# Splitting a fourth head by batch pairs at the end of each convolution layer, with new ring places for the filters

## What is computed

```python
x = x + moe(_gn(x))                    # 8 experts, top 2, silu(x w1) * (x w3) w2
x = x + conv(_gn(x), w3, w7, w15, w_mix)   # three times, own weights
# conv: y = concat([dwconv(x, w) for w in (w3, w7, w15)], axis=channels)
#       y = y.reshape(b, heads, 96, tokens);  out = einsum('blhm,dm->blhd', y, w_mix)
# _gn: mean and variance over a group of 16 tokens x all 512 channels
```

## Time and profile before

| what | value |
|---|---|
| median of 3 runs | 1033.46 us (1033.12 to 1034.08) |
| the profiled execution's own time | 1034.63 us |
| its span in the profile | 1033.0 us |
| PE busy | 992.5 us (96%) |
| DVE busy | 498.2 us (48%) |
| ACT busy | 323.2 us (31%) |
| POOL busy | 255.8 us (25%) |
| mean granted TensorE clock | 0.993 |
| convolution part | about 698 us to the end |

### The profile page before, as it was taken

The page is one execution under the profiler, slowest core; times in us unless marked ns, Lnnn a source line. Parts: engine busy times, 40 slices in busy tenths (PEclk is TensorE's granted clock), DMA queues, the critical chain, the costliest instruction groups (busy, mean ns, idle before and its releaser), DMA issues.

```text
span 1033.0 us, 14467 instructions
## 1 busy us (share of the span) xinstructions
PE 992.5 (96%) x5077; PEld 829.1 (80%) x5078; DVE 498.2 (48%) x660; ACT 323.2 (31%) x437; POOL 255.8 (25%) x359
## 2 busy tenths in 40 slices
PE   4989999999999999999999999968999999999998
PEld 3568888888888888888887888857988898889787
DVE  6763263145136246116337155146733896489411
ACT  2613252144144144125235244122511222122223
POOL 1011112121112112111212111112534245424531
PEclk9999999999999999999999999998999999999999
DMA  9576118934971994981893994975467747674668
GB/s 371 234 263 206 22 30 334 392 107 180 393 259 28 397 393 128 409 303 28 335 389 129 396 376 138 406 222 169 143 204 169 219 143 203 165 223 144 192 152 226
DMA packets 98786, 238.12 MB, mean 231 GB/s; under 512 B 10048, under 2 KB 64576, under 8 KB 83840
## 3 DMA queue, kind: packets, MB, share of 16 engines
q1 hardware_dynamic: 90528, 214.54, 57.6%
q0 software_dynamic: 8080, 23.07, 9.5%
q10 hardware_dynamic: 144, 0.07, 0.0%
HBM read 129.91 MB, written 111.94 MB: 234 GB/s over the span
## 4 chain that ended last, share of the span: by engine, by line
PE 75%; DMA 8%; DVE 6%; issue 5%; SPq 4%; ACT 1%; POOL 0%; ACTq 0%; DVEq 0%; POOLq 0%
PE gate_ps L1020 15%; PE up_ps L1020 15%; PE y_ps L1007 10%; PE head_ps L1598 6%; PE head_ps L1594 6%; PE head_ps L1595 6%; PE y_ps L1010 5%; DMA w_raw<-in_w13T 4%; PE hT_ps L1032 2%; SPq L460 2%; DMA ring<-filters 1%; PE xT_ps L997 1%; DMA rowed<-acc 1%; PE head_ps L1613 1%; PE head_ps L1614 1%
## 5 line engine op out<-in xcount | busy, mean ns | idle before, releaser
L1020 PE MATMUL gate_ps<-front 128*128 128x512 f32 x560 | 176.4, 396 | 2.2 <-DVE xT_lo L867 1.5
L1020 PE MATMUL up_ps<-front 128*128 128x512 f32 x560 | 173.2, 390 | 0.0
L1594 PE MATMUL head_ps<-split,ring 128*128 128x256 f32 (+1 forms) x459 | 158.9, 346 | 4.0 <-DMA ring<-filters 2.4
L1598 PE MATMUL head_ps<-split,ring 128*128 128x256 f32 (+1 forms) x459 | 155.3, 338 | 2.2 <-DVE split L1396 2.2
L1595 PE MATMUL head_ps<-split,ring 128*128 128x256 f32 (+1 forms) x459 | 153.8, 335 | 0.0
L882 DVE TENSOR_TENSOR hidden<-silu,up_ps 128x1024 f32<-128x1024 f32 x35 | 42.7, 1221 | 228.7 <-ACT silu L641 228.7
L1020 PEld LDWEIGHTS up_ps<-front 128*128 128x128 f32 x560 | 105.4, 188 | 22.3
L1020 PEld LDWEIGHTS gate_ps<-front 128*128 128x128 f32 x560 | 102.6, 189 | 22.8 <-DVE front L831 1.8
L528 POOL DMA_INDIRECT acc<-y_row,put x35 | 67.4, 1927 | 214.4 <-ACT y_row L629 214.4
L641 ACT ACTIVATE silu<-gate_ps 128x1024 f32<-128x1024 f32 x35 | 35.9, 1024 | 267.5 <-PE up_ps L1020 267.5
L1007 PE MATMUL y_ps<-w_hi,hT_hi 128*128 128x512 f32 x280 | 112.2, 401 | 1.2 <-ACT hT_hi L623 1.2
(11 more groups left out here) (198 smaller groups left out, 1435.1 us busy)
## 6 DMA issues: line engine op xcount, KB each, us to landing
filters<-rows SPq DMA_DIRECT2D x56, 1568.0 KB
w_raw<-in_w13T SPq DMA_DIRECT2D x32, 1024.0 KB, 16.4
ring<-filters SPq DMA_DIRECT2D x15, 1536.0 KB, 6.6
w_raw<-in_w2T SPq DMA_DIRECT2D x16, 1024.0 KB, 6.0
ring<-filters SPq DMA_DIRECT2D x144, 64.0 KB, 4.1
ring<-filters SPq DMA_DIRECT2D x12, 768.0 KB, 4.8
ring<-filters SPq DMA_DIRECT2D x15, 384.0 KB, 3.7
ring<-filters SPq DMA_DIRECT2D x9, 512.0 KB, 4.0
```

What stands on the lines that cost most here:

```text
L1020: last = nc.tensor.matmul(o[:, n, :], a[:, k, :], b[:, k, t, n * 512:(n + 1) * 512], start=(k == 0 and a is xT_hi and b is w13_hi), stop=( ...
L1594: nc.tensor.matmul(place, kernel_hi, x_hi, start=(u == 0 and a == 0), stop=False)
L1598: nc.tensor.matmul(place, kernel_hi, x_lo, start=False, stop=False)
```

## The change

Head 2 moves from the whole heads to those worked by pairs: the layer's end is now heads 2, 3, 4, 5 for pair 0 and the same for pair 1, 23 tasks in all. `REDUCTIONS` sums heads 0 and 1 whole and heads 2, 3, 4 by pair (one part of three heads where there were two); the totals stand at other tasks; DVE's and ACT's written-out orders have one more `add` and `square` of half a head in the tail, and pair 1's reduction stands behind the third `low`. `RING_PLACE` changes for heads 1 to 5: 1 goes to place 0, 2 to 14, 3 to 19, 4 to 24, 5 to 29. By `RING_AFTER` head 1 then waits for head 8, heads 2 and 3 for head 9, heads 4 and 5 for head 7, and of the next layer head 11 for head 1, head 12 for head 4 of pair 1, head 6 for head 5 of pair 1. The last stores are cut between heads 2 and 3 no more, but between 1 and 2.

```diff
--- before.py
+++ after.py
@@ -91,10 +91,10 @@
 
 
 HEAD_ORDER = (11, 12, 6, 13, 14, 15, 10, 7, 8, 9, 0, 1, 2, 3, 4, 5)
-LAYER_ORDER = ([(h, pair) for pair in range(2) for h in HEAD_ORDER[:3]] + [(h, None) for h in HEAD_ORDER[3:13]]
-               + [(h, pair) for pair in range(2) for h in (3, 4, 5)])
+LAYER_ORDER = ([(h, pair) for pair in range(2) for h in HEAD_ORDER[:3]] + [(h, None) for h in HEAD_ORDER[3:12]]
+               + [(h, pair) for pair in range(2) for h in (2, 3, 4, 5)])
 LAYER_TASKS = len(LAYER_ORDER)
-TAIL = LAYER_TASKS - 6
+TAIL = LAYER_TASKS - 8
 EARLY = 6
 TASKS = [(l, h, pair) for l in range(LAYERS) for h, pair in LAYER_ORDER]
 PIECES = [(j, pair) for pair in range(2) for j in range(1, 7)] + [(j, None) for j in (11, 12, 7, 8, 9, 10, 13, 14, 15, 0)]
@@ -121,7 +121,7 @@
 
 
 RING = 36
-RING_PLACE = {11: 0, 12: 14, 6: 28, 13: 0, 14: 14, 15: 0, 10: 14, 7: 28, 8: 0, 9: 16, 0: 8, 1: 24, 2: 0, 3: 14, 4: 19, 5: 28}
+RING_PLACE = {11: 0, 12: 14, 6: 28, 13: 0, 14: 14, 15: 0, 10: 14, 7: 28, 8: 0, 9: 16, 0: 8, 1: 0, 2: 14, 3: 19, 4: 24, 5: 29}
 HEAD_SEQUENCE = [(l, h) for l in range(LAYERS) for h in HEAD_ORDER]
 RING_AFTER, RING_COUNT = [], []
 for _i, (_l, _h) in enumerate(HEAD_SEQUENCE):
@@ -165,8 +165,8 @@
 SCALED = 2
 SQUARES = 6
 SQUARE_AT = {**{h: h - 10 for h in range(11, 16)}, **{h: h - 6 for h in range(6, 11)}, **{h: h for h in range(5)}, 5: 0}
-REDUCTIONS = ((8, range(11, 16), None), (12, range(6, 11), None), (15, range(0, 3), None),
-              (17, range(3, 5), 0), (18, range(5, 6), 0), (20, range(3, 5), 1), (21, range(5, 6), 1))
+REDUCTIONS = ((8, range(11, 16), None), (12, range(6, 11), None), (14, range(0, 2), None),
+              (17, range(2, 5), 0), (18, range(5, 6), 0), (21, range(2, 5), 1), (22, range(5, 6), 1))
 PARTS = len(REDUCTIONS)
 PART_END = (5, 7)
 SQUARE_AFTER = {h: parts for hs, parts in (((6, 11, 12, 13, 14, 15), 0), ((7, 8, 9, 10), 1), ((0, 1, 2, 3, 4), 2), ((5,), 3))
@@ -177,7 +177,7 @@
 TURNS = {(3, 1): (9,), (3, 2): (10, 11), (4, 1): (12, 13), (4, 2): (14, 15), (5, 1): (16,), (5, 2): (17, 18),
          (6, 1): (19,), (6, 2): (20, 21)}
 STORES = ((9, 11, 16, range(BATCH)), (13, 6, 11, range(BATCH)), (19, 0, 6, range(PAIR)),
-          (19, 0, 3, range(PAIR, BATCH)), (22, 3, 6, range(PAIR, BATCH)))
+          (19, 0, 2, range(PAIR, BATCH)), (23, 2, 6, range(PAIR, BATCH)))
 
 
 def build(nc, x, gate_wT, w13T, w2T, taps, mixT, out):
@@ -1315,15 +1315,16 @@
                 high(0, i)
             for l in range(1, LAYERS):
                 base = (l - 1) * LAYER_TASKS
-                for k in range(TAIL + 3):
+                for k in range(TAIL + 4):
                     square(base + k)
                 root(l, 0)
                 for i in range(2):
                     high(l, i)
-                square(base + TAIL + 3)
+                square(base + TAIL + 4)
                 high(l, 2)
-                square(base + TAIL + 4)
                 square(base + TAIL + 5)
+                square(base + TAIL + 6)
+                square(base + TAIL + 7)
                 high(l, 3)
                 high(l, 4)
                 root(l, 1)
@@ -1479,22 +1480,24 @@
                             reduce(part + r, base + k, heads, pair)
                 add(base + TAIL)
                 add(base + TAIL + 1)
-                reduce(part + 3, base + TAIL + 1, range(3, 5), 0)
                 add(base + TAIL + 2)
-                reduce(part + 4, base + TAIL + 2, range(5, 6), 0)
+                reduce(part + 3, base + TAIL + 2, range(2, 5), 0)
                 add(base + TAIL + 3)
+                reduce(part + 4, base + TAIL + 3, range(5, 6), 0)
+                add(base + TAIL + 4)
                 stats_begin(l, 0)
                 stats_end(l, 0)
                 norm(l, 0)
                 norm(l, 1)
                 low(l, 0)
-                add(base + TAIL + 4)
+                add(base + TAIL + 5)
                 norm(l, 2)
                 low(l, 1)
-                reduce(part + 5, base + TAIL + 4, range(3, 5), 1)
+                add(base + TAIL + 6)
                 low(l, 2)
-                add(base + TAIL + 5)
-                reduce(part + 6, base + TAIL + 5, range(5, 6), 1)
+                reduce(part + 5, base + TAIL + 6, range(2, 5), 1)
+                add(base + TAIL + 7)
+                reduce(part + 6, base + TAIL + 7, range(5, 6), 1)
                 norm(l, 3)
                 norm(l, 4)
                 low(l, 3)
@@ -1630,7 +1633,7 @@
                     for i in TURNS[k, u]:
                         turn(i)
                 if l < LAYERS - 1:
-                    for part, task, unit in ((0, 11, 1), (1, 15, 1), (2, 18, 2), (3, 19, 1), (4, 19, 3)):
+                    for part, task, unit in ((0, 11, 1), (1, 15, 1), (2, 17, 1), (3, 19, 1), (4, 20, 1)):
                         if (k, u) == (task, unit):
                             total(l + 1, part)
                 if l and k == 0 and u >= 2:
```

## The result

The changed kernel takes **1050.59 us** (median of 4 runs, 1049.76 to 1053.71), the kernel before 1033.29 beside it (1031.75 to 1034.08): a ratio of 1.0173, with a 95% interval from 1.0157 to 1.0188, or 17.3 us slower. The forecast was slower by 12.5, with a range up to 1050. The direction holds, and the median lies 0.6 us above the range.

What follows compares the result with a forecast made beforehand. PE, busy 96%, was taken to bound the kernel, with SP's filter issues the narrow place at layer ends. Terms of +3.4, +4.4 and +4.7 us there sum to +12.5, taking 1033.46 to 1046.0 us, range 1041.5 to 1050.

Steps and rivals of the forecast that it cites:

- Which queue, and by how much: At a layer's end SP issues four heads' filters after head 9, not three; head 5's begin at 802.86 instead of 799.10.
- What is given back: After head 5 of pair 1, shorter DVE/ACT waits and head 12's earlier load return 0.65 us per boundary (0.2 to 1.2).
- the first boundary: First layer's end into the next layer: +3.4 us (2.4 to 4.4), as 4.1 less 0.65.
- from head 5 to head 5 of pair 1: Between head 5's pair-0 and pair-1 starts, 14 more matmuls and moved totals turn 7.08 us into 8.0, 0.9 more.
- its twin at the end: Third layer, from head 5 to the last matmul: 14 matmuls and their two transposes add 1.9 us to 8.97.
- a rival with 7%: Layer ends: clock falls in PE's holes, head 5's 20 matmuls take 2.4 us more, three times, giving 1053.2; chance 7%.
- 715 to 720: Profile stretch of the kernel before, cited against a clock fall: clock at 1.00 with PE busy 3.5 of 5 us.
- The holes come singly: PE's holes at layer ends are each at most 3 us with a task between; said against a clock fall.
- Head 13's wait for its load stays: Next layer: head 13's wait hangs on head 11 of pair 1 and on nothing that moves, so it stays.
- The rival of bytes: Layer-end loads are paced by bytes, not issues, so PE would not wait for heads 3 to 5: 1030.8, faster; chance 5%.
- 64 KB to be 0.2 us of data: Small filter DMAs hold no more than 0.2 us of data at 306 GB/s, against 0.6 us an issue.

Runs made afterwards that it cites:

- experiment 1: The kernel before, three split heads, with only the change's new ring places: 1045.26 us, ratio 1.0124.
- experiment 2: The changed kernel, four split heads, with the ring places of the kernel before: 1040.85 us, ratio 1.0061.
- Experiment 3: The changed kernel with 2, 8 and 9 constant matmuls ahead of the filter waits of heads 3, 4 and 5 of pair 0: 1049.67 us, ratio 1.0138.
- experiment 9: The changed kernel with 14 tiny matmuls ahead of the first lane statistics: 1051.66 us, ratio 1.0188.
- experiment 10: The kernel before with 14 tiny matmuls ahead of the first lane statistics: 1035.70 us, ratio 1.0023.
- experiment 11: The changed kernel with 28 tiny matmuls ahead of the first lane statistics: 1056.58 us, ratio 1.0232.
- experiment 4: The changed kernel with the last three DMAs of heads 2 to 5 issued from ACT's queue: 1043.64 us.
- experiment 7: The changed kernel with heads 4 and 5 loaded early from ACT's queue, head 3's last three DMAs from ACT, next layer's head 11 held until head 2: 1040.51 us.
- experiment 5: The kernel of experiment 4 with the next layer's head 11 also held back until head 3 of pair 0 is done: 1043.21 us.
- experiment 6: The changed kernel with the last two DMAs of every head merged into one that reads its source twice: 1053.25 us.

## Why the forecast went wrong, point by point

- **Which queue, and by how much: right.** SP's four blocks begin at 791.78, 795.33, 799.09, 802.86, the forecast's own number, and in the second layer 11.08 us after head 9. The waits before heads 3, 4 and 5 were 0.56, 1.97 and 1.56 us where 0.7, 2 and 2.5 stood (head 4, slowed by the clock, took 0.9 us of the last one), and in the third layer 0, 1.24 and 2.90. Head 5 started at 808.97 where 808.8 to 809.8 stood, in the second layer 3.65 us later for 3.7 to 4.7, in the third 2.40 for 2.3 to 3.3. That the ring places make this queue is shown by experiment 1.
- **What is given back: right at the first boundary, less at the second.** From head 5 of pair 1 to head 13 the step is 0.05 + 0.58, in which 1.33 us of head 13's wait are new; without it 0.70 came back, where 0.65 stood. The wait for DVE inside head 12 is gone at the first boundary and is still there after the second, and at the second only 0.55 came back ahead of head 12, of which 0.22 was left at head 0.
- **The step that failed first: "from head 5 to head 5 of pair 1", and its twin at the end.** The working took all matmuls at 0.118 us. The steps are 2.36 and 2.26 instead of 0.9 each, and 3.51 instead of 1.9. The difference is the clock: head 5 took 4.00, 3.67 and 4.23 us, and 2.48, 2.49 and 2.65 in experiment 2 without the row of holes, 4.3 us in all. Experiment 3 shows that it is the clock and that the holes bring its fall. The forecast had this as a rival with 7%, at 7.2 us; it was not a rival but a further term, at 1.2 to 1.6 a time. The row that misled was 715 to 720, busy for 3.5 of 5 us at a clock of 1.00. It did not hold in the next profile: in the changed kernel's the same wait of 1.48 us for the statistics, in code that the change does not touch, is followed by a low clock in the same 5 us:

```profile
715.00:720.00 5.00, 3.72 (x20) 3.72 (x21) 2.59 (x7) 0.59 (x2) 0.00 (x0) 0.68 0.00 0
```

  So the row was no sign that the clock stays up behind a single wait, and it said nothing of three that follow each other. "The holes come singly" was the wrong sentence.
- **The second: "Head 13's wait for its load stays".** Its load starts where it did, but it met a fetch of PE's instructions: 1.33 us, and 1.53 more because the clock fell behind the longer wait. That is 2.9 of the 4.1 us by which the first boundary (7.46 for 3.4) was missed. Experiments 9 to 11 show it. Since a fetch's place moves with every matmul added to the program, no reading of the change alone would have told the sign; but up to 1.3 us for each load that PE waits for was a bound that belonged in the range.
- **The sum.** 12.5 forecast, and 4.3 of clock at head 5, 2.9 at head 13 make 19.7, against 19.06 in the profile. Both terms are measured in the profiled execution alone, the slowest of four; in the median the miss is 4.8 us, and how it is shared out there is not shown.
- **The rival of bytes** was dismissed for a reason that was only half true. The holes are ended by SP's issues, as its exact times show. But the text took 64 KB to be 0.2 us of data, from a stretch at 306 GB/s, where packets are larger (1.6 KB in the mean). With small ones the engines, busy all the time, moved 247 to 279 GB/s (experiments 4 and 7), and with SP out of the way (experiments 4, 5, 7) the same heads waited for the engines, with 7 to 10 us left of the 17. Of the Trainium skill's sentence in "DMA: Bandwidth & Descriptors", section "Issuing engines are not separate DMA queues", that the initiation is "usually small relative to the DMA itself", these runs say: here the two are of one size, 3.7 us of issues and 2.7 us of packets a head.

Still open: why the packet of instructions moves by 4 us in one place and 7 in another, and why a hole of the same length lowers the clock in one place and not in another (2.6 us before head 5 in the first layer of experiment 1 and 2.7 in the second; 1.48 us before and after, above).

## What to carry to other kernels

When a place table or a buffer is re-cut, write down for every load which task releases it now and count the loads that stand behind the last late release: a table of numbers cost 11.6 us here with no instruction changed. If PE will wait several times in a row, put the loss of clock into the sum (here 1.2 to 1.6 us for 20 matmuls), not among the rivals. And when loads in small packets are late, freeing the issuing queue helps only down to what the DMA engines need for the packets: work out both before building either.

## What the runs showed of the hardware

- A 16 KB packet of the queue "instruction" sat on one of the 16 engines for about 0.9 us in the changed kernel's 842 to 844 us (2.9%), 1.2 in the same stretch of before (3.8%). A load that it falls into lands later: head 13 waited 1.9 to 2.3 us with the packet 2.2 to 4.5 us behind the first issue, 0.8 to 1.1 at 6.2 to 6.9, 0.4 to 0.8 with none in between. At head 5 in experiment 10 it was 0.8 us. One value does not fit (1.68 at 6.2 us, the merged DMA).
- TensorE's granted clock fell to the lower level while PE was busy for 3.25 of 4.52 us, after 1.92 of 3.75 (the first two stretches above), and was back at 1.00 from 813 on, PE having worked head 5 without a break. Behind a wait of 1.48 us in 715 to 720 it was 1.00 in before and 0.68 in the changed kernel. Behind single holes of up to 1.8 us in experiment 2 it stayed up; behind 1.9 to 2.3 before head 13 it fell in the changed kernel and in experiments 2, 7 and 9, and not in 4, 5 and 6.
- Small packets, 0.5 KB in the mean, cost an engine 34 ns each (5176 in 791.8 to 807.1 us), and 344 of 2 KB cost 87 ns each (93.7% of 16 engines' 2 us, 842 to 844 us), so four times the bytes for 2.6 times the time. By an estimate from the first figure 16 engines move near 240 GB/s of small packets (0.5 KB by 34 ns, times 16); full stretches showed 247 to 279, and 360 with the larger ones.
